# A convolution and a windowed linear attention on one core: q in single passes for pairs of tiles, its projection in q's bank, the pooled q placed by VectorE

## What is computed

```python
x = x + conv3x3(group_norm(x), w)                       # layer 0
h = windows_4x4(group_norm(x))                          # layer 1: 196 windows of 16 tokens
qkv = h @ qkv_w.T                                       # 768 channels
pooled = avg_pool5(qkv)                                 # within each 4x4 window, / 25
q, k, v = heads_of(concat(qkv, pooled))                 # 64 heads of 8
q, k = relu(q), relu(k)
out = q @ (k.T @ [v, 1])                                # linear attention in each window
out = out[..., :-1] / (out[..., -1:] + 1e-15)
x = x + batch_norm(out @ proj_w.T)
```

## Time and profile before

| what | value |
|---|---|
| median of 3 runs | 2419.68 us (2418.15 to 2420.84) |
| the profiled execution | 2419.14 us, span 2417.3 us |
| granted TensorE clock, mean | 0.999 |
| PE busy, share of the span | 98% |
| DVE, ACT, POOL busy | 72%, 60%, 48% |
| the chain that ended last | PE 95%, DVE 2%, issue 1% |

### The profile page before, as it was taken

One profiled execution on the slowest core, in us unless ns is written; L12 is line 12 of the kernel. 1 busy time (PEld: TensorE's weight loads), 2 busy tenths in 40 slices (PEclk: granted clock), 3 DMA queues, 4 the chain that ended last, 5 costly groups with the idle time before them and its releaser, 6 DMA issues.

```text
span 2417.3 us, 112385 instructions
## 1 busy us (share of the span) xinstructions
PE 2366.7 (98%) x49576; PEld 2150.9 (89%) x49576; DVE 1730.8 (72%) x3206; ACT 1451.0 (60%) x3754; POOL 1170.9 (48%) x2365
## 2 busy tenths in 40 slices
PE   7999999999999999999999999999999999998998
PEld 7998899888998889988899888998889988897887
DVE  9887658767587765877658766687766876665764
ACT  2158861588516884178832788327882288813886
POOL 0037750477405773057730677216771167712776
PEclk9999999999999999999999999999999999999999
DMA  4000010000200001000010000100001000000000
GB/s 171 1 2 16 19 65 10 2 19 16 75 1 6 15 20 71 1 6 19 16 71 1 7 18 16 71 1 9 16 20 66 1 9 19 21 9 2 16 16 25
DMA packets 39114, 58.37 MB, mean 24 GB/s; under 512 B 4704, under 2 KB 36064, under 8 KB 36832
## 3 DMA queue, kind: packets, MB, share of 16 engines
q1 hardware_dynamic: 38880, 55.27, 6.4%
HBM read 29.57 MB, written 25.69 MB: 23 GB/s over the span
## 4 chain that ended last, share of the span: by engine, by line
PE 95%; DVE 2%; issue 1%; DMA 0%; ACT 0%; SPq 0%; POOL 0%; POOLq 0%; DVEq 0%
PE ps L354 33%; PE ps L425 15%; PE ps L373 12%; PE ps L414 10%; PE ps L400 9%; PE ps L380 9%; PE ps L389 4%; PE ps L434 3%; DVE dp L883 1%; DMA xs<-w_conv 0%; PE ps L336 0%; DVE xs L896 0%; DVE kv_part L989 0%; PE ps L365 0%; DVE rcp L999 0%
## 5 line engine op out<-in xcount | busy, mean ns | idle before, releaser
L354 PE MATMUL ps<-dp,wc 128*128 128x392 f32 x4608 | 840.8, 341 | 0.2 <-DVE dp L883 0.2
L354 PEld LDWEIGHTS ps<-dp,wc 128*128 128x128 f32 x4608 | 815.3, 188 | 5.3 <-issue 3.1
L1204 POOL TENSOR_TENSOR ve<-vpraw,vmask 128x1024 f32<-128x1024 f32 x200 | 381.0, 1905 | 349.8 <-ACT vpraw L665 349.8
L425 PEld LDWEIGHTS ps<-at,wp 128*128 128x128 f32 x3200 | 373.1, 191 | 47.5 <-DVE kvm L1016 46.4
L425 PE MATMUL ps<-at,wp 128*128 128x128 f32 (+1 forms) x3200 | 404.7, 280 | 1.0 <-ACT yb L700 1.0
L1175 POOL TENSOR_TENSOR qm<-qraw 128x64 f32<-128x64 f32 x200 | 59.5, 298 | 700.5 <-ACT qraw L672 699.9
L636 ACT CAST dp<-dt 128x896 fp32r<-128x896 f32 x128 | 121.0, 945 | 449.0 <-PE ps L354 356.3
L373 PE MATMUL ps<-wkv,xt 128*128 128x512 f32 x1200 | 324.8, 406 | 1.6 <-issue 1.6
L654 ACT ACTIVATE ve<-ps,vmask 128x256 f32<-128x256 f32 x800 | 314.3, 491 | 0.0
L414 PEld LDWEIGHTS ps<-kvm,qs 64*32 64x32 f32 x25088 | 233.5, 105 | 90.8 <-issue 88.8
L1016 DVE TENSOR_TENSOR kvm<-ps,hm 128x576 f32<-128x576 f32 (+1 forms) x400 | 277.4, 734 | 2.9 <-PE ps L400 2.8
(11 more groups left out here) (86 smaller groups left out, 3110.3 us busy)
## 6 DMA issues: line engine op xcount, KB each, us to landing
out<-xs SPq DMA_DIRECT2D x224, 112.0 KB, 1.8
xs<-x SPq DMA_DIRECT2D x14, 1344.0 KB, 7.5
xs<-x SPq DMA_DIRECT2D x14, 224.0 KB, 2.7
xs<-w_conv SPq DMA_DIRECT2D x2, 1152.0 KB, 12.2
xs<-x SPq DMA_DIRECT2D x2, 896.0 KB, 6.6
xs<-x SPq DMA_DIRECT2D x2, 672.0 KB, 7.8
kvm<-w_kv SPq DMA_DIRECT2D x1, 512.0 KB, 13.7
wp<-w_proj SPq DMA_DIRECT2D x4, 128.0 KB, 9.9
```

The costliest lines, as they stand in the source:

```text
L354: last = nc.tensor.matmul(ps[:, conv_bank(v, mt), 0:CONV_N], wc[:, part_w, k, kt * TAPS + dy, mt * P:(mt + 1) * P], dp[:, kk % 2, part_d, ...
L425: last = nc.tensor.matmul(ps[:, BANK_A + mt, Y0:Y0 + n], wp[:, q, mt * P:(mt + 1) * P], at[:, q, e, 0:n], start=(q == 0), stop=(q == QUADS ...
L1204: nc.gpsimd.tensor_tensor(ve[:, t % 2, :, 1].rearrange("p e (n m) -> p e n m", m=DIM + 1)[:, :, :, 0:DIM], vpraw[:].rearrange("p (n m) -> ...
```

## The change

q is computed for two tiles at a time. Its weights `wq` and the tokens `xt` now have high and low parts as k and v have, so that `q_of_pair` (L381) is twelve fp32r matmuls of 256 columns in place of twice four float32 matmuls of 128. It stands in the even turns; ACT copies the pair's q out of the bank once (`qraw`), places q of each tile from that copy, and POOL sums the pair's q at once, with instructions twice as long. The half tile at the end has a pass of 64 columns of its own.

The projection goes to q's bank 0 (`BANK_Q`). In odd turns it is divided: channels 0 to 127 stand where q was, behind `keys_times_values`, and channels 128 to 255 behind `pooled`. In even turns it stays whole, behind `pooled`.

The pooled q is placed by DVE (`pooled_q`, L1057) in place of ACT: for tile s+1 in turn s behind the two masks, and for tile 0 ahead of turn 0, behind `tile_low` of tile 3. Some products at the image's ends use other banks; the product that stood in the last turn between `attend` and `turn` now stands behind `turn`. Alignments in front of the loop and behind it have other offsets.

```diff
-            def q_of_tile(e):
+            def q_of_pair(tokens=2 * TT):
                 for mt in range(MT):
-                    for kt in range(KT):
-                        last = nc.tensor.matmul(ps[:, BANK_Q, mt * TT:(mt + 1) * TT],
-                                                wq[:, kt, mt * P:(mt + 1) * P], xh[:, e, kt, :],
-                                                start=(kt == 0), stop=(kt == KT - 1))
+                    for i, (part_w, part_x) in enumerate(PARTS):
+                        for kt in range(KT):
+                            last = nc.tensor.matmul(
+                                ps[:, BANK_Q, mt * 2 * TT:mt * 2 * TT + tokens],
+                                wq[:, part_w, kt, mt * P:(mt + 1) * P],
+                                xt[:, part_x, kt, :, :].rearrange("p e t -> p (e t)")[:, 0:tokens],
...
                 if half and s == 0:
-                    pe.wait_ge(q_ready, n2)
+                    pe.wait_ge(qraw_ready, pairs - 1)
                     product(*half)
-                elif is_tile(2):
-                    pe.wait_ge(q_ready, n2)
-                    q_of_tile(e)
-                elif half:
-                    pe.wait_ge(q_ready, n2 if is_tile(1) else n1)
+                if e == 0:
+                    if is_tile(2) and s != 0:
+                        if is_tile(3):
+                            pe.wait_ge(xh_low, n4)
+                        pe.wait_ge(y_ready, n0)
+                        q_of_pair(2 * TT if is_tile(3) else TT // 2)
+                elif is_tile(-1):
+                    pe.wait_ge(qraw_ready, pairs)
+                    if is_tile(-2):
+                        pe.wait_ge(y_ready, n0)
+                    project(1 - e, 2, (0,) if is_tile(2) else range(MT))
+                if half and s == TILES - 2:
+                    pe.wait_ge(masked, masks)
                     product(*half)
                 pe.wait_ge(ao_ready, n1)
                 turn(units(0))
                 if is_tile(2):
                     pooled(n3)
...
+                if e == 1 and is_tile(-1) and is_tile(2):
+                    project(1 - e, 2, (1,))
...
+                if half and s == TILES - 1:
+                    product(*half)
...
-            def pooled_q(b, t):
-
-                act.wait_ge(qsum_ready, b * TILES + t + 1)
-                if t >= 2:
-                    act.wait_ge(att_done, b * TILES + t - 1)
-                for a in range(2):
-                    last = nc.scalar.activation(
...
+            def pooled_q(b, t):
+
+                dve.wait_ge(qsum_ready, b * PAIRS_Q + t // 2 + 1)
+                if t >= 2:
+                    dve.wait_ge(att_done, b * TILES + t - 1)
+                n = tile_units(t) * TT // 2
+                for a in range(2):
+                    last = nc.vector.tensor_scalar(
...
             def attention(b):
                 normalize_tile(b, 3)
                 tile_low(b, 3)
+                pooled_q(b, 0)
...
                     if s + 1 < TILES:
                         mask(b, s + 1, 0)
                         mask(b, s + 1, 1)
+                        pooled_q(b, s + 1)
...
             def normalize_tile(b, t):
 
                 if t >= 2:
-                    dve.wait_ge(q_done, b * TILES + t - 1)
                     dve.wait_ge(xh_high, b * TILES + t - 1)
```

More of the change, by code:

```diff
@@ L419, in attend, with project @@
                 last.then_inc(att_done, 1)
-            def project(e, units):
+            def project(e, units, mts=range(MT)):
                 n = units * TT // 2
-                for mt in range(MT):
+                for mt in mts:
                     for q in range(QUADS):
-                        last = nc.tensor.matmul(ps[:, BANK_A + mt, Y0:Y0 + n],
+                        last = nc.tensor.matmul(ps[:, BANK_Q, mt * TT:mt * TT + n],
                                                 wp[:, q, mt * P:(mt + 1) * P], at[:, q, e, 0:n],
                                                 start=(q == 0), stop=(q == QUADS - 1))
-                last.then_inc(proj_done, 1)
+                if mt == MT - 1:
+                    last.then_inc(proj_done, 1)
             def turn(units):
@@ L436, in turn, with tile @@
                     last.then_inc(tr_done, 1)
-            def tile(T, e, s=None, v=None):
+            def tile(T, pair, e, s=None, v=None):
                 def is_tile(d):
@@ L448, in tile @@
                 n0, n1, n2, n3, n4 = [held(pe, T + d) for d in range(5)]
-                masks, own_mask = held(pe, T * 2 + 2), held(pe, T * 2 + 3)
+                masks, pairs = held(pe, T * 2 + 2), held(pe, pair + 1)
+                half = None if v is None else {0: (v - 1, 1), TILES - 3: (v, 0), TILES - 2: (v, 1),
+                                               TILES - 1: (v + 1, 0)}.get(s)
                 pe.wait_ge(w_loaded, DMA)
@@ L483, in tile @@
                     pooled(n3)
[L484 to L489, removed]
+                if e == 1 and is_tile(-1) and is_tile(2):
+                    project(1 - e, 2, (1,))
+                if s == 0:
+                    if half:
+                        pe.wait_ge(conv_added, 2 * v + 4)
+                    pe.wait_ge(xh_low, n4)
+                    pe.wait_ge(qraw_ready, pairs - 1)
+                    q_of_pair()
+                if half and s == TILES - 1:
+                    product(*half)
+                if e == 0 and is_tile(-1):
+                    if is_tile(2):
+                        pe.wait_ge(qraw_ready, pairs)
                     else:
@@ L523, in attention @@
                 for s in range(FIRST_LOOPED):
-                    tile(t0 + s, s % 2, s, v)
+                    tile(t0 + s, p0 + s // 2, s % 2, s, v)
                 at_slot(SLOT_LOOP)
@@ L561, in later_chunks @@
                             continue
-                        if b >= 1 and (c, kk) == (2, 0):
-                            pe.wait_ge(y_ready, b * TILES + 1)
                         product(v, 0)
@@ L750, in first_chunk @@
                 keys_values(b, 0)
-                q_of_tile(b, 0)
                 pooled_keys_values(b, 0)
                 split(v + 4)
+                q_of_pair(b, 0)
                 split_tile(b, 2)
                 keys_values(b, 1)
+                for t in range(2):
+                    q_of_tile(b, t)
                 pooled_keys_values(b, 1)
@@ L1221, in _ @@
             for b in range(B):
+                spread_pooled(b, 0)
                 pool_q(b, 0)
-                spread_pooled(b, 0)
                 spread_pooled(b, 1)
-                for s in range(-1, TILES):
-                    if 0 <= s < TILES - 2:
+                for s in range(TILES):
+                    if s < TILES - 2:
                         spread_pooled(b, s + 2)
-                    if s + 2 < TILES:
-                        pool_q(b, s + 2)
+                    if s % 2 == 0 and s + 2 < TILES:
+                        pool_q(b, s // 2 + 1)
                     if 1 <= s:
```

131 lines of the change are left out of this document (74 added, 57 removed).

## The result

| kernel | median us | lowest to highest | ratio to before |
|---|---|---|---|
| before (5 runs beside it) | 2419.68 | 2418.15 to 2420.84 | 1 |
| changed | 2496.38 | 2483.96 to 2499.24 | 1.0313, 95% interval 1.0289 to 1.0338 |

The change costs 77 us; 24 were forecast. The profiled execution took 2483.96 us (span 2481.9), the shortest of five, so its trace shows 65 us of the 77 (2481.9 - 2417.3). Its mean granted clock is 0.995, that of the four others 0.991 to 0.993, where the kernel before has 0.999.

A forecast was written before the change was run, and what follows sets the result against it. PE, busy 98% of the span, was taken to bound the kernel. Terms -29 + 4 + 8 + 21 + 24 - 4 = +24 us gave 2443 us, with a range of 2410 to 2467.

The forecast's parts named there:

- q in pairs: On PE: twelve fp32r matmuls per pair replace two tiles' q; gain 0.16 to 0.46 us a pair, 29 us in all.
- The half tile: q of the half tile, twelve records of 64 columns: 0.48 us more, 8 times, a loss of 4 us.
- The start: First `attend` of each image waits for DVE's placing of tile 0: 2.6 us, 8 times, a loss of 21 us.
- The last turn: Turn 24 of seven images: `turn` waits 1.13 us for DVE's division, the product now behind it; a loss of 8 us.
- Placing in the loop: DVE's second placing meets POOL's spread in two of three odd turns, `attend` waiting 0.45 us: a loss of 24 us.
- These are the ends, 6 and 36: Bounds of the loop's loss: 6 us if the normalisation is caught instead of the placing, 36 if every odd turn's placing is.
- In an even turn the spread comes 0.5 to 0.7 later [...] and the placing passes: Even turns: longer q and ACT's copy delay POOL's spread, so DVE's placing escapes it.
- Turn 2: Turn 2 of seven images: `pooled`'s 0.66 us wait for DVE shrinks as q is about 0.5 longer; 4 us gained.
- the start was not hidden: Rival: the wait at the attention part's start is hidden; 2404 us with no catch, 2422 with two in three; chance 0.13.
- a pair's q takes 1.5 us: Rival: the 256-column pass runs at float32 rate, a pair taking 5.7 us and the program 2850; chance 0.03.
- neither none nor all were caught: Two rivals on odd turns meeting the spread: every one caught, 2455 us, chance 0.20; none caught, 2425 us, chance 0.16.

The follow-up runs named there:

- the short spread: Changed kernel, but POOL spreads the pooled v into one of four places, the others keeping zeros (also called the quarter spread): 2437.18 us.
- the run that makes them early, with ACT placing: Changed kernel with ACT placing the pooled q, the two last turns as before, and tile 0's masks ahead of a convolution input: 2412.83 us.
- the run with the placing alone: Kernel before, with only DVE placing the pooled q; q, projection and POOL's sums as before: 2456.66 us.
- first placing earlier: Changed kernel, with DVE's placing for tile 0 ahead of the normalisation of tile 3 instead of behind its low part: 2479.26 us.
- The version with 2403 us: Changed kernel with ACT placing, last two turns as before, tile 0's masks early, and DVE's normalisation of tile s+4 ahead of the masks: 2402.58 us.
- ACT placing and ends as before: Changed kernel with ACT placing the pooled q, the two last turns as before, tile 24's placing ahead of turn 23's copies: 2417.37 us.

## Why the prediction was wrong

The direction was right, the size was not: 77 us in place of 24.

- **q in pairs**, forecast 0.30 us a pair: right. Without placings on DVE, or with the short spread, 18 turns take 132.8 to 133.8 us in place of 136.1, 0.25 to 0.37 a pair, 24 to 35 us if all 96 pairs gain as much.
- **The half tile**, forecast +0.48: its block takes 1.36 us (1252.24 to 1253.60), 0.27 more than q's 1.09; 2 us.
- **The start**, forecast 2.6 us: right, 22.8 us in eight waits, of which some 4.6 are the later masks (2417.4 - 2412.8, the run that makes them early, with ACT placing). What follows it was not seen: falls of the clock, about 1 us each.
- **The last turn**, forecast 1.13: right, 8.4 us more in `turn`'s waits. The turn ahead of it was not looked at. There the projection now stands ahead of the product, so nothing lies between `turn` and the next `attend`, which waits 0.6 us for ACT's copy. Undoing both gave 14 us.
- **Placing in the loop**, forecast +24: this step failed. For the placings themselves, place and way were right: in 28 of the 80 odd turns of the loop the first placing met an add of POOL and took 0.43 to 0.59 us, the second began 0.04 to 0.12 us behind the spread and was caught, and the `attend`s behind them waited 42.5 - 22.8 = 20 us. That this lies near 24 is luck: there were fewer catches than two in three, and each cost 0.7 us in place of 0.45. What was wrong is the sentence "These are the ends, 6 and 36", which took the caught placing and the caught normalisation as alternatives and priced the second at 6 us, and with it "In an even turn the spread comes 0.5 to 0.7 later [...] and the placing passes": it passes, and the normalisation behind it is caught instead. Nearly every turn has one of the two, and behind the caught normalisations `pooled` waits 23 us in turns 3 to 20 alone. The quarter spread measures the loop's loss as 59 us by the medians, 50 by the 18 turns of the eight images (6.3 x 8).
- **Turn 2**, forecast -4: right, the wait of `pooled`'s weight loads is down from 0.90 us (0.66 of PE's own wait) to 0.36. But the wait for "issue" of turn 1 reappears in turn 2 (1.28 us), and at the loop's exit others grew: 8 us more at `attend`.

With the sizes of the traces the sum is -35 + 2 + 23 + 8 + 5 + 50 - 4 + 8 = +57. The falls of the clock add about 1 us in each of three turns 0 and 1.6 at the end of the fourth image (a product of 5.01 us in place of 3.44): 62, where the two spans differ by 65. The 12 us by which the median of the changed kernel lies above its profiled execution stand in no trace; the granted clock was lower there. The terms are not independent: undoing the ends gave 14 us beside DVE's placing and 26 beside ACT's, where ACT's placing of tile 24 stood between the copy and `attend`. None of the rivals holds: the start was not hidden, a pair's q takes 1.5 us (1141.27 to 1142.80), and of the odd turns neither none nor all were caught.

## What to carry to other kernels

An instruction put ahead of others on an engine costs what it delays, not what it lasts: 0.6 us of placing moved the normalisation behind it into a 2 us instruction of another engine. List for each moved instruction what stands behind it, where that will now fall, and who is behind that in the next engine's list. And when work is taken out from between a producer and its reader, look at both turns that it touches.

## What the runs showed of the hardware

- A wait of PE can cost twice. After the waits before the first `attend` (2.9 us, 2.2 in the last image) the granted clock fell in four of eight images; in the run with the placing alone, after 2.2 us, in three (0.66 over 5 us); after waits of 1.2 us (first placing earlier) in none. The version with 2403 us has 0.994 to 0.998 in its executions and runs 2400 to 2411; that with the early masks takes 2410 us at 0.998 and 2416.6 at 0.994.
- A small recorded lead, by which DVE's instruction starts ahead of the spread, doesn't decide alike for all instructions. The second placing of 1144.99 starts 0.05 us ahead of the spread and takes 0.34 us, as do all 67 placings of the trace with a lead of up to 0.12; a normalisation with 0.06 lost, and in the changed kernel seven lost with 0.09 to 0.11. All that lost with a lead, in both traces, stood right behind another normalisation; 19 that stood behind another kind passed with 0.08 to 0.10. Why, no run shows.

```profile
1144.99 0.34 DVE L1057 TENSOR_SCALAR qs<-qsum,qmaskp 128x256 f32<-128x256 f32 x1
```

- Four instructions of 256 elements on POOL take 641 ns each, where one of 1024 takes 1.99 us: with 2.3 to 2.5 us for the four, the split loses 0.3 to 0.5.
- `attend` waits 16.5 us before and up to 37.3 us (ACT placing and ends as before) for "issue", at the same places of each image and up to 2.2 us long. By the Trainium skill (Runtime: NRT & Kernel Launch, Instruction fetch mechanics) the step from one block of instructions to the next is mostly hidden. If these waits are such steps, the trace does not agree; what they are was not shown, and other offsets changed nothing in the time.
